# Routing blocks 0 and 1 of the second expert layer inside the retention layer, with their scatters issued during its last batch

## What is computed

```python
x = x + time_mix(layernorm(x))
x = x + ffn(layernorm(x))                  # expert layer, first use
x = x + retention(layernorm(x))            # 16 heads, 4 batches of 1024 tokens
x = x + ffn(layernorm(x))                  # expert layer, second use

def ffn(x):                                # E = 64 experts, F = 64, K = 4 choices
    logits = flat @ router_w
    _, topk_idx = top_k(logits + router_bias, K)
    weights = softmax(logits) at topk_idx, scaled to a sum of 1
    routed = sum of the 4 chosen experts' (silu(x @ wg) * (x @ wu)) @ wd, weighted
    shared = (silu(x @ swg) * (x @ swu)) @ swd      # every token
    return routed + shared
```

## Time and profile before

| | us |
|---|---|
| three runs | 1761.79, 1759.8, 1764.59 |
| median | 1761.79 |
| span of the profiled execution | 1770.5 |
| time_mix, in that execution | 0 to 197 |
| first expert layer: route, experts | 197 to 465, 465 to 655 |
| retention | 655 to 1089.7 |
| second expert layer: route | 1089.7 to 1334.9 |
| second expert layer: experts and sum | 1334.9 to 1770.5 |

### The profile page before, as it was taken

How to read it: one execution, slowest core, us unless ns; L and a number is a source line. 1 busy time by engine, 2 the same in 40 slices (tenths; PEclk the granted TensorE clock), 3 DMA queues, 4 the chain that set the end, 5 groups by cost and what they waited for, 6 DMA issues and landing times. The chain is left out here.

```text
span 1770.5 us, 24406 instructions
## 1 busy us (share of the span) xinstructions
PE 1348.5 (76%) x7408; PEld 924.2 (52%) x7408; DVE 1091.4 (62%) x2773; ACT 687.1 (39%) x1466; POOL 921.4 (52%) x1063
## 2 busy tenths in 40 slices
PE   6686656788699986998688985638876777777775
PEld 2344523455588873564456564325544555555533
DVE  5899755556366662473777775725654655555558
ACT  5998201111366652424133613111214444544420
POOL 3999364554555546656636032663453555555520
PEclk9898577889899998999799997869888888888878
DMA  9800531121788876112111003521136444443168
GB/s 363 343 1 0 201 136 56 71 86 61 207 276 265 271 250 185 57 46 69 39 53 39 3 1 128 219 101 49 68 97 185 148 140 140 140 134 105 40 238 272
DMA packets 109395, 233.81 MB, mean 132 GB/s; under 512 B 21543, under 2 KB 43470, under 8 KB 108756
## 3 DMA queue, kind: packets, MB, share of 16 engines
q1 hardware_dynamic: 81076, 164.03, 27.6%
q0 software_dynamic: 27648, 68.23, 11.3%
q10 hardware_dynamic: 544, 0.00, 0.0%
HBM read 125.44 MB, written 115.11 MB: 136 GB/s over the span
## 5 line engine op out<-in xcount | busy, mean ns | idle before, releaser
L882 POOL DMA_INDIRECT slots_x<-arena,slot x256 | 258.2, 1009 | 207.7 <-DVEq L981 131.4
L1248 POOL DMA_INDIRECT pairs_y<-arena x192 | 189.1, 985 | 177.2 <-DVE arena L1319 117.4
L1167 PE MATMUL moe_narrow<-arena 128*128 128x128 f32 x1536 | 232.7, 301 | 8.0 <-DVE arena L1311 6.7
L1311 DVE TENSOR_TENSOR arena<-arena,moe_narrow 64x128 f32<-64x128 f32 x384 | 111.6, 291 | 205.2 <-ACT arena L1215 186.3
L1167 PEld LDWEIGHTS moe_narrow<-arena 128*128 128x128 f32 x1536 | 212.9, 215 | 16.7 <-issue 15.0
L1156 PE MATMUL moe_narrow<-ident,arena 128*128 128x128 f32 x768 | 137.7, 308 | 92.8 <-ACT arena L1209 68.3
L707 PE MATMUL moe_wide<-arena 128*128 128x512 f32 x384 | 190.7, 644 | 22.0 <-DVE arena L1002 22.0
L1209 ACT ACTIVATE arena<-moe_narrow 128x512 f32<-128x512 f32 x192 | 114.6, 597 | 197.7 <-remote 117.8
L456 POOL DMA_INDIRECT arena<-slots_y,slot x128 | 128.7, 1005 | 87.0 <-DMA arena<-slots_y,slot 46.6
L1156 PEld LDWEIGHTS moe_narrow<-ident,arena 128*128 128x128 f32 x768 | 93.7, 155 | 146.8 <-issue 143.8
L799 ACT ACTIVATE arena<-moe_wide 128x512 f32<-128x512 f32 x48 | 28.7, 598 | 319.0 <-PE moe_wide L707 153.7
(11 more groups left out here) (318 smaller groups left out, 2410.4 us busy)
## 6 DMA issues: line engine op xcount, KB each, us to landing
arena<-slots_x SPq DMA_DIRECT2D x192, 264.0 KB, 3.8
slots_x<-arena SPq DMA_DIRECT2D x48, 528.0 KB, 15.8
slots_y<-arena SPq DMA_DIRECT2D x96, 256.0 KB, 3.7
arena<-w_gu SPq DMA_DIRECT2D x2, 8192.0 KB
arena<-pairs_y SPq DMA_DIRECT2D x32, 512.0 KB, 5.7
residual<-x SPq DMA_DIRECT2D x8, 512.0 KB
arena<-sw_gu SPq DMA_DIRECT2D x4, 1024.0 KB
slots_x<-arena,slot POOLq DMA_INDIRECT x256
```

What stands on the lines that cost most here:

```text
L882: pool.indirect_dma_start(out=x_slots, in_=xn[:, t, :], in_offset=None, out_offset=bass.IndirectOffsetOnAxis(ap=slot[:, t, i:i + 1], axis=0))\
L1167: last = pe.matmul(h_ps[n % 2][:, j * P:(j + 1) * P], weights[:, n % 3, j, h, :], xt[:, n % XTRING, (j * KH + h) * P:(j * KH + h + 1) * P] ...
L1248: pool.indirect_dma_start(out=slots.y_of, in_=ytile[:, n % YRING, j, :], in_offset=None, bounds_check=slots.pairs - 1, oob_is_err=False, o ...
```

## The change

`FirstBlock` becomes `FirstBlocks` and routes blocks 0 and 1 to the end. In the transition to the last batch, PE now transposes both blocks and makes both logits (in one bank, `sc[1]`) ahead of `group_sum(b, 0)`; ACT copies both transposes and keeps the logits of both in SBUF (`keep_logits`), from which `choose` and `pick_gates` now read; DVE does `choose(0)`, `choose(1)`, `places` and `slots_of` of both blocks (`slots_of` of before is split into these two), with the slots of block 1 among the output additions. `pick_gates` of both blocks and `statistics(3)` go behind `chunks(3)`. POOL numbers the rows of these blocks (`number_pairs`) and issues their 32 scatters: 16, a power, 10, then `group_power`, then 6 and a power. The route of "moe2" begins with block 2: `DONE = 2`, its rows and logits first, then the transposes of blocks 0 and 1 (for the shared expert alone), and scatters of blocks 2 to 7 only. The loop over FB is unchanged. A table `turn_of` gives the place of a block in the new order to the semaphores of the transposes.

```diff
 def experts(...):
-    DONE = 1 if first else 0
+    DONE = first.ROUTED if first else 0
+    order = [DONE] + list(range(DONE)) + list(range(DONE + 1, NB))
+    turn_of = {n: at for at, n in enumerate(order)}
...
         def route_tensor(pe):
             if first:
-                pe.sem_inc(sem("lg_full"), 1)
-                pe.sem_inc(sem("ranked"), 1)
-                transposes(1, 0)
-                transposes(1, 1)
...
-            logits(1)
-            transposes(2, 0)
-            transposes(2, 1)
-            pe.wait_ge(sem("shared_w"), 32)
-            gate_up(0, 0)
-            rank(1)
-            logits(2)
-            gate_up(0, 1)
-            rank(2)
+                pe.sem_inc(sem("lg_full"), DONE)
+                pe.sem_inc(sem("ranked"), DONE)
+                transposes(2, 0)
+                transposes(2, 1)
+                pe.wait_ge(sem("rw"), 16)
+                logits(2)
+                for n in range(DONE):
+                    transposes(n, 0)
+                    transposes(n, 1)
+                pe.wait_ge(sem("shared_w"), 32)
+                gate_up(0, 0)
+                rank(2)
+                gate_up(0, 1)
...
         def route_scalar(act):
+                normalise(2)
+                for n in (2, 0, 1):
+                    keep_transposes(n, 0)
+                    keep_transposes(n, 1)
+                keep_logits(2)
+                silu(0, 0)
+                normalise(3)
+                silu(0, 1)
...
         def route_gpsimd(pool):
                 pool.sem_inc(sem("moments_ready"), SEEN)
+                power(SEEN, SEEN + 2)
-            for n in range(NB):
+            for n in range(DONE, NB):
...
-                if n == 0 and first:
-                    power(SEEN, NB)
+                if n == DONE and first:
+                    power(SEEN + 2, NB)
...
         def route_vector(dve):
-                for n in range(SEEN, NB):
-                    statistics(n)
-                choose(1)
-                slots_of(1)
+                statistics(4)
+                statistics(5)
+                choose(2)
                 multiply(0, 0)
-                choose(2)
+                slots_of(2)
                 multiply(0, 1)
-                slots_of(2)
-                pick_gates(1)
+                statistics(6)
+                statistics(7)
...
 class FirstBlocks:
+    def scatter(self, pool, n, turns):
+        pool.wait_ge(self.sem("first_numbers"), 1)
+        pool.wait_ge(self.sem("first_xn"), self.BLK * (n + 1))
+        pool.wait_ge(self.sem("first_slots"), n + 1)
+        for at in turns:
+            t, i = self.BLK * n + at // self.K, at % self.K
+            pool.indirect_dma_start(out=self.k.slots.x, in_=self.xn[:, t, :], in_offset=None,
+                                    out_offset=bass.IndirectOffsetOnAxis(ap=self.k.slot[:, t, i:i + 1], axis=0))\
+                .then_inc(self.landed[n], 16)
...
 def retention(...):                       # PE, ending
-                    first.transposes(pe, sc[1:3])
+                    first.transposes(pe, 0, sc[1:3])
                 project(b + 1, 0, range(CH))
                 if ending:
-                    first.logits(pe, sc[1])
+                    first.transposes(pe, 1, sc[1:3])
                 project(b + 1, 0, range(CH, 2 * CH))
+                if ending:
+                    first.logits(pe, 0, sc[1])
+                    first.logits(pe, 1, sc[1])
                 group_sum(b, 0)
...
                 project(b + 1, 1, range(5))
+                if ending:
+                    first.rank(pe, 1, sc[2])
                 group_sum(b, 1)
...
         def _(pool):
-                if b == B - 2:
-                    first.power(pool, powers_made, 2, 4)
+            pool.wait_ge(sem("added"), 2 * choices.K * (TB // 2 * (B - 1) + BLK // 2))
+            first.number_pairs(pool)
+            first.scatter(pool, 0, range(BLK * choices.K))
+            first.power(pool, powers_made, 2, 3)
+            first.scatter(pool, 1, range(10))
             group_power(B - 1)
+            first.scatter(pool, 1, range(10, BLK * choices.K))
+            first.power(pool, powers_made, 3, 4)
...
         def _(dve):                       # b == B - 2
-                    first.choose(dve, looking, sc[1])
+                    first.choose(dve, looking, 0)
                     mean(b)
                     keep_values(b + 1, 0)
-                    first.pick_gates(dve, looking, sc[1])
-                    first.slots_of(dve, looking, sc[2])
+                    first.choose(dve, looking, 1)
+                    first.places(dve, looking, 0, sc[2])
+                    first.slots_of(dve, looking, 0)
                     variance(b)
                     gate(b)
                     keep_values(b + 1, 1)
+                    first.places(dve, looking, 1, sc[2])
+                    output(b, range(2))
+                    first.slots_of(dve, looking, 1)
+                    output(b, range(2, TB // 2))
                     first.statistics(dve, looking, 2)
-                    first.statistics(dve, looking, 3)
-                    output(b)
...
             chunks(B - 1)
+            first.pick_gates(dve, looking, 0)
             sum_rows(B - 1)
             mean(B - 1)
+            first.pick_gates(dve, looking, 1)
             variance(B - 1)
             gate_last(B - 1)
+            first.statistics(dve, looking, 3)
             output(B - 1)
```

251 lines of the change are left out of this document (158 added, 93 removed).

## The result

The changed kernel takes **1777.88 us** (median of 13 runs, 1765.65 to 1789.21), the kernel before 1761.79 (13 runs, 1756.86 to 1771.28): ratio **1.0086**, 95% interval 1.0064 to 1.0107. It is slower by 15 to 16 us, where I forecast 19 us faster; it lies outside my range. The profiled execution spans 1779.3 us against 1770.5, which is 8.8 longer.

The account below looks back on a forecast made before the run. The route of "moe2" was taken as bound by waits between engines, 31.6 us a block; -33 + 3.7 + 10 + 0.5 = -18.8 us gave 1751.7 profiled, 1743 median, forecast range 1737 to 1753, outer range 1732 to 1760.

Parts of the forecast that it names:

- chunks(3): State-update loop of the last batch, beside 26 scatters: loses 10 us, between a lower bound of 3.4 and 15 to 17.
- the transition: Relay of PE and DVE into the last batch: first masked product 3.7 us later, 3 to 6 possible.
- the route: Route of "moe2" without blocks 0 and 1: 33 to 37 us shorter at 31.6 us a block; 33 taken.
- Rival 3: Route does not keep its pace, gains only 16 us from the earlier loop start: 1759.5 us; chance 0.09.
- the gathers' 3.4: Lower bound for the last batch's loop: 23 held-back gathers cost chunks(1) 3.4 us, 26.8 against 23.4.
- rival 2: PE held for most of the scatter bursts in chunks(3), loss up to 34 us: 1767 us; chance 0.16.
- That sign: Stretch of 14 state updates in chunks(3), 33 us forecast; prediction wrong if it leaves 27 to 40 us.
- rival 4: POOL held by DVE in chunks(3), scatters 1.6 us each, late to group_power: 1747 to 1751 us; chance 0.05.
- The end of retention: Two pick_gates and one statistics behind chunks(3) fit into existing waits: nothing, at most 1 us; 0.5 in the sum.

Follow-up runs that it names:

- gathers_free_b: Kernel before, with gathers of retention's batches 1 to 3 no longer waiting for the landing of the one two before; on the 1762 us chip: 1799.38 us, ratio 1.0244.
- slots_late_b: Changed kernel, block 1's last slot steps moved out of the transition, its 16 scatters to the route's start; on the 1762 us chip: 1771.70 us, ratio 1.0079.
- bias_late: Changed kernel, with POOL's output bias addition for the last batch moved behind the 26 scatters; on the 1762 us chip: 1775.70 us, ratio 1.0087.
- places_behind: Changed kernel, with DVE's places(1) moved behind the output additions and block 2's statistics; on the 1532 us chip: 1542.08 us, ratio 1.0062.
- scatter_in_route: Changed kernel, with the 32 scatters of blocks 0 and 1 moved from retention to the route's start; on the 1532 us chip: 1548.87 us, ratio 1.0106.
- both_moved: Changed kernel, with the 32 scatters at the route's start and places(1), slots_of(1) behind output additions and statistics; on the 1532 us chip: 1547.68 us, ratio 1.0094.
- both_moved_b: both_moved run again on the 1762 us chip, one run: 1785.96 us.
- one_at_a_time: slots_late_b's kernel, with each block 0 scatter issued only after the one before landed, 12 ahead of the last group_power; on the 1762 us chip, one run: 1759.63 us.

## Why the prediction was wrong

**The sum.** Against the forecast of -18.8 the four terms missed by +13.1 (`chunks(3)`), +9.0 (the transition), +2.9 (the route) and +2.1 (the end); with +0.5 from the parts that the change doesn't touch that makes the +8.8 of the profiles. `chunks(3)` alone would have left the change 5.7 us faster, in my own terms; it took the transition as well to make it slower, and 1777.88 lies above all my rivals' ranges.

**The route, -33 forecast, -30.1 measured: right by the profile that I worked from, in part by luck.** The first burst came 31.1 us behind the route's start (31.3 forecast), the pace was 32.1 us (31.6 forecast). Rival 3 falls. But the unchanged route itself took 237.6 us in gathers_free_b, and against that the gain is 22.5.

**`chunks(3)`, +10 forecast, +23.1 measured: the term that failed most.** I had seen the effect and called for it in the sum, but sized it from late answers in the route (9.0 for a burst of 16, scaled) and chose the middle to the gathers' 3.4. Both ends were bad measures. The late answer of a `down` is the delay of that one result, begun in mid-burst, where the whole relay of the loop is late by nearly the burst, as far as the burst stands beside it: 16.0 of 17.8 us in slots_late_b, 23.1 of 24.4 in the changed kernel. And the gathers' 3.4 was the price of gathers with pauses; without them they cost 23.1 us more (49.9 against 26.8 for the state updates). This was rival 2, which I had at 0.16 with a loss of up to 34. The stretch of state updates took 39.4: between the 33 of the forecast and the "over 43" of rival 2, and just inside the 27 to 40 beyond which I had called myself wrong. That sign was badly chosen: 7.1 of the 23.1 us fell ahead of the first state update, which came 10.3 us behind the first masked product instead of 3.2, where the sign did not look.

**The thought that was missing** stands across two steps. The 31.6 us a block, from which I took the gain of 33, are a burst with PE held plus the rest; on Y, where nothing holds PE, the route loses only 7.9 us by the same edit. So most of the route's gain on X goes with what only X has. The same 32 were put where every step of the loop needs PE, and hold it there. I took the gain at full price and the cost at less than half.

**The transition, +3.7 forecast, +12.7 measured (+13.0 on Y).** The first half was right: ahead of `variance` the relay got 3.1 us longer (29.5 to 32.6 from the row sums on, 3.6 forecast), and DVE came just in time (1.13 us of waiting left). The second half failed. I wrote 3.8 + 4.4 + 2.7 us for 5.3 and booked none of the 5.6 between them, as if PE's output matmuls would cover it; DVE was the late one, and PE sat idle for 11.57 us ahead of the second half of these matmuls. From the variance to the first masked product it took 9.3 us more. And `places(1)` took 13.4 us with its PSUM steps instead of 3.8, since it stands beside POOL's decays and bias addition. For the bias addition bias_late shows it (3.94 to 0.43 us, T 4.0 less); for the decays it is read from the durations, 1.2 us each beside multiplications of 1.25. The Trainium skill says so in "SBUF — State Buffer", § SBUF: two separate sides: a VectorE operation with two inputs in SBUF and a GpSimd operation that reads SBUF lock each other out of the shared port pair for the whole instruction. The trace agrees: 3.94 us beside the 3.81 us of L2344 and 0.43 without it; the additions that read PSUM, 0.69 us beside POOL's decays in places_behind and 0.69 without them, are not held. Steps with one input were held too: L1737 for 1.19 us, L1624 in places_behind for 4.00. I had read that page for the scatters (rival 4, which fell: they took 0.96 us) and not for the step that I put beside POOL's arithmetic.

**The end of retention, +0.5 forecast, +2.6 measured.** Without the six scatters E is 22.9 to 23.0 (scatter_in_route, both_moved and both_moved_b), with them 25.0 to 25.2 (the change alone, places_behind, bias_late), where before it was 22.1 to 22.6: the `pick_gates` nearly fitted into the waits, the scatters behind `group_power` did not, on Y either. How they cost the 2 us there is not shown.

**Not forecast and not explained:** 5.4 us ahead of the transition and -4.9 in the experts. Ahead of the transition no step of the change stands that DVE would pass, and profiles on X spread from 953.7 to 967.5 at that point, so I take it as the spread between executions. On Y the experts took 336.6 and 338.3. The profiles' +8.8 and the medians' +16.1 differ because the profiled execution lies 8.7 us above the median before and 1.4 above it after.

**Still open:** why X and Y differ, and what in X makes a row of indirect DMAs hold PE. The pauses lie between matmuls, for which the profile shows no releaser; whether PE is kept from SBUF there or from its next instruction no view here tells. PE was held with scatters 1.27 and 1.35 us apart and not with one in flight, 2.7 apart; whether the number in flight or the pace decides is open. The page of the Trainium skill that the prediction cites, "SBUF — State Buffer", says in § Who interferes with whom that TensorE never waits on anyone. Y's traces agree (C 28.8 with 26 scatters); in X's PE is late beside POOL's DMAs (52.0), though it isn't shown that it waits at SBUF. Not tried: one scatter in flight in the route itself, and one_at_a_time with more than one execution. Its single time is 1759.63 against a median of 1759.13, with a first part 14 us longer than in the profile of the kernel before. Its T, C, E and R add up to 361.2 us, against 381.2 in that profile and 377.2 in gathers_free_b's: a hint that it gains on X, and not a result.

## What to carry to other kernels

Where work is moved that slows a neighbour, its effect moves along: price it in the place where it goes by the same rows that give the gain in the place that it leaves. A relay in which every step needs an engine loses nearly the whole time for which that engine is held (23.1 of 24.4 us here), not the lateness of one answer. Where POOL's indirect DMAs stand beside a loop that needs PE, try them with one in flight before moving them, look at how long DVE's small steps take beside POOL's arithmetic, and measure on more than one chip.

## What the runs showed that I had not expected

- Two kinds of chip ran the same program in 1762 and 1532 us, and a one-line edit (the gathers' pauses) is worth -0.49% on one and +2.44% on the other. `chunks(3)` without scatters took 28.9 us on both; the route (245.2 and 184.8) and the experts (435.6 and 336.6), which have POOL's indirect DMAs in them, differ by 60 and 99 us.
- On the first, a row of 26 scatters 1.27 us apart made a loop of 28.9 us take 52.0; 1.35 us apart, 45.5; twelve 2.7 us apart with one in flight, 29.0.
- Over such a row PE's granted clock was 0.60, against 1.00 over the state updates of the kernel before. It was at the lower level already (0.51 from 1038 to 1046, PE idle) and was there while PE got single matmuls (0.50 from 1065.0 to 1079.3). The clock does not make the loss: at 0.50 the 32 matmuls of L2051 take 1.96 us in a row, and in the row of scatters they took 14.2. Over the whole row 94 matmuls are recorded in 34.6 us, where 354 took 23.4 us before.

```profile
1046.10:1080.70 34.60, 22.23 (x94) 13.07 (x94) 15.61 (x38) 0.77 (x2) 26.63 (x28) 0.60 0.27 98
```

```profile
1041.40:1064.80 23.40, 23.40 (x354) 18.10 (x349) 21.42 (x44) 6.05 (x30) 0.00 (x0) 1.00 0.01 1
```
